# TensorE's order in cross attention, from one unit at a time to pairs of units

## What is computed

```
x = layernorm(x + linear_attention(x))              # 16 heads of 8
x = layernorm(x + cross_attention(ctx, x))          # 16 heads of 64
x = layernorm(x + mixture_of_experts(x))            # 8 experts, 2 chosen, and a shared one

cross_attention(ctx, lat), for each sequence:
  q = norm(lat) @ Wq                                # 128 queries
  k, v = split(concat(norm(ctx), norm(lat)) @ Wkv)  # 120 + 128 = 248 keys
  out = softmax(q k^T / 8) v                        # for each head
  return out @ Wout
```

## Time and profile before

| | |
|---|---|
| median of 3 runs | 2010.5 us |
| the profiled execution, its own time | 2006.77 us |
| its span, first to last instruction | 2004.7 us |
| mean granted TensorE clock | 0.990 |
| TensorE matmuls (PE) busy | 1945.1 us (97%) |
| VectorE (DVE) busy | 1490.9 us (74%) |
| ScalarE (ACT) busy | 1277.6 us (64%) |
| GpSimd (POOL) busy | 1287.5 us (64%) |

### The profile page before, as it was taken

The page is one execution under the profiler, slowest core; times in us unless marked ns, Lnnn a source line. Parts: engine busy times, 40 slices in busy tenths (PEclk is TensorE's granted clock), DMA queues, the critical chain, the costliest instruction groups (busy, mean ns, idle before and its releaser), DMA issues. The chain is left out here.

```text
span 2004.7 us, 47352 instructions
## 1 busy us (share of the span) xinstructions
PE 1945.1 (97%) x15995; PEld 1683.6 (84%) x15995; DVE 1490.9 (74%) x3901; ACT 1277.6 (64%) x3929; POOL 1287.5 (64%) x1461
## 2 busy tenths in 40 slices
PE   8999979999999999999999999999999989999997
PEld 5565569999999999999999999899999977888875
DVE  6999956777777777777777778777777755555675
ACT  4777656666666666666666666666666655555565
POOL 5888766666666666666666666666666655444674
PEclk9999989999999999999999999999999998999999
DMA  5101000000000000000000001000000012222454
GB/s 167 44 19 30 17 19 8 11 17 16 16 15 22 15 17 16 16 15 23 14 18 16 16 15 32 25 18 16 16 14 17 10 41 63 85 86 81 127 147 142
DMA packets 103984, 75.27 MB, mean 38 GB/s; under 512 B 10998, under 2 KB 97638, under 8 KB 103622
## 3 DMA queue, kind: packets, MB, share of 16 engines
q1 hardware_dynamic: 94806, 54.20, 9.7%
q0 software_dynamic: 8640, 17.97, 2.5%
q10 hardware_dynamic: 304, 0.07, 0.0%
HBM read 39.64 MB, written 32.57 MB: 36 GB/s over the span
## 5 line engine op out<-in xcount | busy, mean ns | idle before, releaser
L1193 POOL TENSOR_TENSOR x_prob<-x_prob,x_inv 128x496 f32<-128x496 f32 x512 | 519.6, 1015 | 460.1 <-DVE x_inv L1312 457.4
L1258 ACT ACTIVATE x_prob<-x_ps_S,x_nmax 128x248 f32<-128x248 f32 x1024 | 471.1, 468 | 224.1 <-DVE x_nmax L1306 222.2
L1306 DVE TENSOR_REDUCE x_nmax<-x_ps_S 128x2 f32<-128x496 f32 x512 | 343.0, 670 | 105.8 <-PE x_ps_S L1064 97.7
L1273 ACT COPY x_probT<-x_ps_T 124x512 f32<-124x512 f32 x512 | 300.3, 587 | 166.7 <-PE x_ps_T L1455 164.3
L1062 PE MATMUL x_ps_S<-first_kT_lo,x_G_hi 128*128 128x248 f32 x1024 | 327.4, 320 | 0.0
L1455 PE MATMUL x_ps_T<-ident,x_prob 128*124 128x128 f32 x2048 | 319.0, 279 | 8.4 <-POOL x_prob L1193 7.1
L1455 PEld LDWEIGHTS x_ps_T<-ident,x_prob 128*124 128x124 f32 x2048 | 233.1, 141 | 74.4 <-POOL x_prob L1193 28.3
L1064 PE MATMUL x_ps_S<-first_kT_hi,x_G_hi 128*128 128x248 f32 x1024 | 284.5, 278 | 0.0
L1063 PE MATMUL x_ps_S<-first_kT_hi,x_G_lo 128*128 128x248 f32 x1024 | 284.2, 278 | 0.0
L1425 PE MATMUL x_ps_O<-x_probT,x_V 124*64 124x128 f32 x4096 | 251.9, 276 | 0.0
L1292 DVE TENSOR_TENSOR x_G_lo<-x_ps_G,x_G_hi 128x512 fp32r<-128x512 f32 x256 | 176.0, 687 | 89.0 <-ACT x_G_hi L1252 88.9
(11 more groups left out here) (263 smaller groups left out, 4419.9 us busy)
## 6 DMA issues: line engine op xcount, KB each, us to landing
w_wkv<-sorted_rows SPq DMA_DIRECT2D x142, 66.0 KB
e_back<-sorted_results SPq DMA_DIRECT2D x32, 256.0 KB, 3.5
latents<-first_nlat SPq DMA_DIRECT2D x32, 128.0 KB, 1.8
turned_rows<-w_rows SPq DMA_DIRECT2D x32, 128.0 KB, 1.8
w_wq<-turned_rows SPq DMA_DIRECT2D x32, 128.0 KB, 2.3
out_dram<-e_result SPq DMA_DIRECT2D x16, 256.0 KB, 2.4
first_nk<-latents SPq DMA_DIRECT2D x32, 124.0 KB
first_nk<-in_ctx SPq DMA_DIRECT2D x32, 120.0 KB, 2.3
```

The lines of the kernel that those rows point to most:

```text
L1193: nc.gpsimd.tensor_tensor(prob[:, k], prob[:, k], inv[:, k].unsqueeze(2).broadcast_to([P, 2, K]), ALU.mult).then_inc(prob_ready, 1)
L1258: nc.scalar.activation(prob[:, k, h, :], ps_S[:, n % BANKS, h * K:(h + 1) * K], ACT.Exp, bias=nmax[:, k, h:h + 1], accum_out=total[:, k, h ...
L1273: nc.scalar.copy(probT[0:KT, s % (2 * GANG)], ps_T[0:KT, s % 2, :]).then_inc(probT_ready, 1)
L1306: nc.vector.tensor_reduce(nmax[:, k, :], ps_S[:, n % BANKS, 0:2 * K].rearrange("p (h k) -> p h k", h=2), AX, ALU.max, negate=True).then_in ...
```

## The change

TensorE's body is written by pairs of units instead of units. The other engines' queues are as they were.

```diff
-            def weighted_values(g):
+            def weighted_values(g, made):
...
                 for k in range(GANG):
                     j, u = g * 2 + k // 2, k % 2
+                    if k == GANG - 1:
+                        pe.wait_ge(probT_ready, made + GANG)
...
-                pe.wait_ge(probT_ready, n * GANG + GANG)
+                pe.wait_ge(probT_ready, n * GANG + GANG - 1)
                 if g % 2 == 0:
                     pe.wait_ge(V_ready, r * 8 + 4 + g * 2)
                 wait(pe, outT_ready, n)
-                weighted_values(g)
+                weighted_values(g, n * GANG)

+            def turn_weights(unit, s):
+
+                pe.wait_ge(prob_ready, unit + s + 1)
+                if unit + s > 1:
+                    pe.wait_ge(probT_ready, unit + s - 1)
+                for h in range(2):
+                    for tile in range(2):
+                        at = (h * 2 + tile) * S
+                        last = nc.tensor.transpose(ps_T[0:KT, s % 2, at:at + S], prob[:, s % RINGS, h, tile * KT:(tile + 1) * KT],
+                                                   ident[:])
+                last.then_inc(T_psum, 1)
+
+            def first_half(r, par, j):
+
+                unit, s, ahead = r * UNITS, 2 * j, j + 3
+                turn_weights(unit, s)
+                if s % GANG == 0 and unit + s:
+                    if s == 12 and r:
+                        pe.wait_ge(slots.shifted_ready, r)
+                    if s == 4 and r > 1:
+                        pe.wait_ge(routed, (r - 2) * STEPS + SLOT_STEP)
+                    gang_output(r * GANGS + s // GANG - 1)
+                if s == 4 and r < FINAL:
+                    pe.wait_ge(V_ready, r * 8 + 4 + 2)
+                    first.turn_keys(pe, ps_V, ident, r + 1, 1 - par)
+                if r < FINAL or j + 1 < PAIRS:
+                    scores((unit + s + LEAD) % BANKS, 1, par if j + 1 < PAIRS else 1 - par, (j + 1) % 2)
+                if r < FINAL or ahead < PAIRS:
+                    pe.wait_ge(G_lo_ready, r * PAIRS + ahead)
+                    if s == 10:
+                        pe.wait_ge(kT_lo_ready, r + 2)
+                    make_G(ahead % 2, par if ahead < PAIRS else 1 - par, ahead % PAIRS)
+                if s == 2 and r > 1:
+                    pe.wait_ge(outT_ready, r * GANGS)
+                    slots.ranks(pe, ps_O, r - 2)
+                if s == 2 and r:
+                    pe.wait_ge(V_ready, r * 8 + 5)
+                    output(r - 1)
+                if s == 10 and r:
+                    slots.logits(pe, ps_O, r - 1)
+
+            def second_half(r, par, j):
+
+                unit, s, ahead = r * UNITS, 2 * j + 1, j + 2
+                if r < FINAL or ahead < PAIRS:
+                    pe.wait_ge(exp_ready, (unit + s + 1) * 2)
+                    pe.wait_ge(G_lo_ready, r * PAIRS + ahead + 1)
+                    scores((unit + s + LEAD) % BANKS, 0, par if ahead < PAIRS else 1 - par, ahead % 2)
+                if r < FINAL or j < 4:
+                    if s == 3 and r:
+                        pe.wait_ge(sum_ready, r)
+                    elif s == 5 and r < FINAL:
+                        pe.wait_ge(kT_ready, r + 2)
+                    else:
+                        pe.wait_ge(V_ready, r * 8 + 4 + j)
...
+                    make_V(par if j < 4 else 1 - par, 1 - j // 4, j % 4 // 2, j % 2)
+                if s == 9 and r:
+                    pe.wait_ge(outT_ready, r * GANGS + 2)
+                    slots.turn_rows(pe, ps_O, ident, r - 1)
+                turn_weights(unit, s)

+                for j in range(PAIRS):
+                    first_half(r, par, j)
+                    second_half(r, par, j)
```

More of the change, by code:

```diff
@@ L1436, in gang_output @@
                 wait(pe, outT_ready, n)
-                weighted_values(g)
-            def body(r, par):
[L1440 to L1496, removed]
@@ new lines, in second_half @@
+            def second_half(r, par, j):
[11 more added lines that the diff above has]
+                        pe.wait_ge(V_ready, r * 8 + 4 + j)
+                    if s == 9:
+                        pe.wait_ge(kT_lo_ready, r + 2)
+                    make_V(par if j < 4 else 1 - par, 1 - j // 4, j % 4 // 2, j % 2)
[3 more added lines that the diff above has]
+                turn_weights(unit, s)
```

## The result

| | before | after |
|---|---|---|
| median of the runs beside each other | 2010.33 us (2008.28 to 2011.55, 4 runs) | 2123.28 us (2122.45 to 2123.99, 4 runs) |
| ratio, 95% interval | | 1.056 (1.0544 to 1.0576) |
| the profiled execution, its own time | 2006.77 us | 2122.62 us |
| its span | 2004.7 us | 2120.5 us |
| mean granted TensorE clock | 0.990 | 0.988 |

The order by pairs makes the kernel 113 us slower. The clock isn't the reason for the 113 us: it is 1.00 in the stage on both sides. I locate the time by TensorE's transpositions. The stage's first one starts at 278.7 us (before: 279.6) and its last one at 1750.9 (1641.5), so the stage is 110 us longer. What lies behind it takes 369.6 us against 363.2; more on those 6 us at the end.

The account below looks back on a forecast made before the run. TensorE's own stream was taken to bound cross attention (busy 1359.63 of 1369 us). New waits 107.9, less 12.1 of present waits, plus 3 for gangs: +98.8 on 2006.8, with 3.7 to the median 2109 us, range 2068 to 2140.

Parts of the forecast that it names:

- (a): T(0'), next round's first transposition, waits 1.52 us for VectorE's queue from G(1') on: 7.76 against TensorE's 6.24.
- (b): V at step 5 waits 0.55 us a round for VectorE's keys, queued behind maxima and inverse that need S(7).
- (c): Rows' transposition (L293) waits 0.92 us for GpSimd's L243 (3.73), second bound out_copy (3.52); 0.19 already there.
- (d): Logits wait 0.24 us for ScalarE's L281, behind T(9)'s copy and unit 12's exponentials; ends 0 and 0.4.
- (e): T(8) waits by a chain from the keys through VectorE's queue; taken as 0.3 us, bounds 0 and 0.8.
- V at step 3: V at step 3 waits for the residual, 0 to 0.1 us, costed at nothing.
- the two waits of before: Present waits at T(0') (0.20) and the rows' transposition (0.19), together 0.39 us a round, counted as gone: 12.1 us.
- three gangs followed by S: Gang to S instead of gang to T in three gangs of four: 0.03 us each, 3 us, ends 0 and 8.
- the rival with 1977 us: Faster: T-to-S crossings cost TensorE 0.085 us each, so fewer save 22 us and present waits go; 4%.
- The forecast's case of 12 us for one more change between T and gang: If T to gang were one more mode change of 0.09 us, the sum would be 128 x 0.09 = 12 us higher.
- The slower-by-half rival: One wait relieves the others, so only some 1.6 us a round is lost: 2060 us; 13%.
- The four thin covers: T(2), T(6), T(12), T(14) have 0.3 to 0.5 us to spare; breaking adds 37 us, 2146; 8%.

Follow-up runs that it names:

- seven: Changed kernel with keys, second normalise and gang's copy each a step earlier, logits behind S(14), routing spread over steps 12 to 15: 2032.56 us, ratio 1.0111.
- eight: Kernel before (order by units) with GpSimd's second normalise (L243) at step 7 and routing spread 13: 3, 14: 3, 15: 9: 2001.06 us, ratio 0.9944.
- three: Changed kernel with VectorE's out_copy one step earlier, at step 4m ahead of routing and maxima: 2105.73 us, ratio 1.0469.
- four: Changed kernel with five of the nine routing operations of VectorE's steps 13 and 14 moved to step 15: 2101.21 us, ratio 1.0445.
- Six: Changed kernel with GpSimd's second normalise (L243) at step 7 and out_copy at step 4m, behind routing and ahead of the maxima: 2066.66 us, ratio 1.027.
- five: Changed kernel with VectorE's two keys operations moved from step 5 to step 4, ahead of maxima(7): 2115.99 us, ratio 1.0523.
- two: Kernel before (order by units) with only the gang and the keys' transpositions moved between T(s) and S: 2096.24 us, ratio 1.0423.

## Why the prediction was right

The forecast was 2109 us with 2068 to 2140; 2123 came. It was the likeliest case, slower by five waits of TensorE, short by 14 us. By its steps, in us per round (a measured figure includes the slower start of the block that waited, where it has one):

| step | forecast | measured |
|---|---|---|
| (a) T(0') | 1.52 | 1.60 |
| (b) V at step 5 | 0.55 | 0.58 |
| (c) rows' transposition | 0.92 | 0.88 |
| (d) logits | 0.24 | 0.27 |
| (e) T(8) | 0.30 | 0.29 |
| V at step 3 | 0 | 0.10 |
| the two waits of before | 0.39 | 0.52 |
| three gangs followed by S | 0.09 | 0.14 |

**The stream.** S starts 0.354 behind T and the next block 0.77 behind that S, together 1.12, before and after. In the change T beside T takes 0.435 and S alone 0.69, which is 1.125 without a crossing. Nothing was saved by fewer crossings, so the rival with 1977 us is out, by the timelines and by experiments seven and eight. The Trainium skill, "TensorEngine Tiling (Array Packing)", Key Properties, says that a change of the tiling mode drains TensorE. The trace agrees as to the places: an extra of 0.09 is at the gang's start in both orders, 0.055 to 0.10 where T or S follows it, and crossings between T, S, G and V have none. That the extra is such a drain no run shows. The forecast's case of 12 us for one more change between T and gang is out: the gang starts 0.095 late behind T and 0.093 late behind G.

**The gangs.** The price not seen before, gang to S, is 0.047 more than gang to T (0.10 of extra against 0.055), inside the bounds of 0 and 0.08 and above the 0.03 taken: 96 x 0.047 = 4.5 us for 3.

**(a)** is right in chain and size: 7.76 for 7.76. The 0.08 missing is 0.03 of stream and 0.05 between this round and the mean. Experiments three and four show that it is VectorE's queue: what is moved in it moves T(0').

**(b)** is the keys. The timelines of after at step 5, TensorE:

```profile
935.56 0.36 PE L1062 MATMUL x_ps_S<-first_kT_lo,x_G_hi 128*128 128x248 f32 x1
...
938.21 0.49 PE L1062 MATMUL x_ps_V<-first_wv_lo,first_kT_hi 128*124 128x512 f32 x1 [0.32 <-DVE first_kT_full L561]
938.54 0.40 PE L1063 MATMUL x_ps_V<-first_wv_hi,first_kT_lo 128*124 128x512 f32 x1
938.78 0.40 PE L1064 MATMUL x_ps_V<-first_wv_hi,first_kT_hi 128*124 128x512 f32 x1
```

and VectorE:

```profile
936.53 0.67 DVE L1306 TENSOR_REDUCE x_nmax<-x_ps_S 128x2 f32<-128x496 f32 x1 [2.76 <-PE x_ps_S L1064]
...
937.20 0.51 DVE L560 TENSOR_SCALAR first_kT_full<-x_ps_V,w_gain 128x240 f32<-128x240 f32 x1
937.62 0.53 DVE L561 TENSOR_SCALAR first_kT_full<-x_ps_V,w_gain 128x256 f32<-128x256 f32 x1
```

S(7) starts at 935.56 and V at 938.21, 2.65 later (forecast 2.67); 0.97 of it up to the maxima. TensorE's own way there is 2.17 (forecast 2.12), so V waits 0.48, and its second matmul follows 0.33 behind the first instead of 0.23. Only with these 0.10, for which the forecast had no term, is it 0.58.

**(c)** has two chains of nearly one length, which end together. After, GpSimd:

```profile
948.67 0.79 POOL L243 TENSOR_SCALAR w_rows<-slots_hsum,slots_mom,slots_rstd 128x128 f32<-128x128 f32 x1
```

VectorE:

```profile
948.78 0.68 DVE L1302 COPY x_outT<-x_ps_O 128x512 f32<-128x512 f32 x1
```

and TensorE behind both:

```profile
948.51 0.40 PE L1064 MATMUL x_ps_V<-first_wv_hi,first_kT_hi 128*124 128x512 f32 x1
949.61 0.41 PE L293 MATMUL x_ps_O<-ident,w_rows 128*128 128x128 f32 x2 [0.70 <-DVE x_outT L1302]
```

L243 ends at 949.46 and the copy at 949.46; the trace names the copy, and in 4 rounds GpSimd. The forecast put its two bounds 0.21 apart, 3.73 and 3.52, but only the first holds the 0.15 from the last operation to the matmul: like for like it had them 0.06 apart. Experiment three moved the copy out of the way, and the wait rose to 1.29, now for GpSimd's L243 in all 28 rounds. Six moved both, and it went; no run moves GpSimd's operation alone in this order.

**(d) and (e)** are right in place, and partly by luck in size. (d) is 0.16 of wait and again 0.10 of a slower start behind it, for a forecast of 0.24 of wait. (e) wasn't walked: 0.3 was picked between 0 and 0.8, and 0.29 came. How much it hangs on its neighbours is seen in experiment five (0.65) and two (0.66 in two parts).

**What was mis-sized.** No step fell; the sum was short. In the stage it was 98.8 us and 110.2 came (1472.2 against 1362.0 from the first to the last transposition). Per round the forecast's terms make 3.53 + 0.09 - 0.39 = 3.23, and the measured ones 3.72 + 0.14 - 0.52 = 3.34, while the round grew by 3.49. The surplus of 0.26 is: V at step 3, 0.10, which stood there as "0 to 0.1" and was costed at nothing (V starts on time, its second matmul comes 0.33 behind the first); the five waits together 0.09; the gangs 0.05; less 0.13, because the present waits, read off single rows as 0.20 and 0.19, are 0.30 and 0.22 in the mean of the rounds; and 0.15 that is in no row of the table, of which 0.11 are the gangs behind T(0') and T(8): a gang starts 0.055 later behind a T that has waited. Taken by kind, the five waits themselves were forecast with 3.53 and measured with 3.41; what the forecast put at nothing are the slower starts behind them and of V at step 3, 0.42 together. The surplus is 8 us in 31 rounds; 3.4 more lie in the first and last rounds. The last 2.5 us of the 14 are not in this stage, see the last section.

**The slower-by-half rival** had a core of truth that the change itself doesn't show: waits do relieve each other. Five and seven show it when they are taken away (0.58 gives 0.22). It didn't lower the sum: the forecast had taken (e) with (b) in place. The four thin covers held in the change, within 0.01 us; T(6) broke in seven, T(2) by 0.12 in four.

## What to carry to other kernels

On an engine that is busy for all of a stage, moving a long block from behind to ahead of the operations that feed the others cost next to nothing in its own stream (0.05 us a gang here) and much through theirs: they idle during the block and are late afterwards, and it waits for them (T(0') 1.6 us). So walk each in-order queue back from the producer of each block, at its new place, and compare with the stream. If an order is changed, the other engines' queues have to be fitted anew; and the same search for waits of some tenths in the old order gave 0.6% here for two small edits, a time that the new order didn't reach.

## What the runs showed of the hardware

The same program's experts' part takes 363.2, 367.2 us (before, two executions), and 368.1 to 370.3 in the ten others, though in cross attention the round repeats to 0.01. In eight, ScalarE shows one stall there for which the trace names no engine of the core:

```profile
1672.70 0.32 ACT L1760 ACTIVATE e_silu<-e_ps_gu 128x176 f32<-128x176 f32 x1 [3.32 <-remote]
```

The change has one such of 4.0 us, the second execution of before one of 2.1, and the first one of before none. So 4 us come and go with the execution of one and the same program. That all ten others lie above both executions of before is not explained, and what the stall waits for I can't tell. Such a profile can be lucky by 4 us; the forecast corrected it by the 3.7 to the median, the comparison of two profiles doesn't.

A block behind a wait can cost more than the wait. V's first at step 5 starts at 938.21 and its second 0.33 later, against 0.24 from there to the third, so V there takes 0.80 instead of 0.69. A wait is to be read from the spacing of starts, not from the figure that the trace prints beside it (1.40 where the spacing gives 1.99 - 0.44 = 1.55 at T(0')).
